# Last cross attention of a four-layer stack on one core: exponentials in a ring of six units, products with the values by halves behind later scores

## The reference, cut to what matters

```python
def _L3_xattn_ref(input, encoded_features, Wq, bq, Wkv, bkv, Wo, bo):
    B, T, E, H = (2, 256, 128, 16)
    D = E // H
    b, tq, _ = input.shape
    tk = encoded_features.shape[1]
    q = (input @ Wq + bq).reshape(b, tq, H, D).transpose(0, 2, 1, 3)
    kv = (encoded_features @ Wkv + bkv).reshape(b, tk, 2, H, D).transpose(2, 0, 3, 1, 4)
    k, v = (kv[0], kv[1])
    scores = jnp.einsum('bhqd,bhkd->bhqk', q, k) / math.sqrt(D)
    attn = jax.nn.softmax(scores, axis=2)
    out = jnp.einsum('bhqk,bhkd->bhqd', attn, v)
    out = out.transpose(0, 2, 1, 3).reshape(b, tq, H * D)
    return out @ Wo + bo
...
x = x + jnp.tanh(g_xattn[3]) * _L3_xattn_ref(_layernorm(x, axis=-1), ctx_1024, L3_xattn_Wq, ...)
```

## Time and profile before

| | |
|---|---|
| median of 3 runs | 1386.9 us (1382.16 to 1395.86) |
| the profiled execution: its own time | 1379.55 us |
| its span in the profile | 1377.7 us |
| TensorE's granted clock over the span | 0.972 of full speed |
| PE busy | 1249.3 us (91%) |
| DVE busy | 977.7 us (71%) |
| ACT busy | 932.6 us (68%) |
| POOL busy | 741.9 us (54%) |

### The profile page before, as it was taken

One profiled execution on the slowest core, in us unless ns is written; L12 is line 12 of the kernel. 1 busy time (PEld: TensorE's weight loads), 2 busy tenths in 40 slices (PEclk: granted clock), 3 DMA queues, 4 the chain that ended last, 5 costly groups with the idle time before them and its releaser, 6 DMA issues. The chain is left out here.

```text
span 1377.7 us, 44878 instructions
## 1 busy us (share of the span) xinstructions
PE 1249.3 (91%) x17964; PEld 892.8 (65%) x17964; DVE 977.7 (71%) x2439; ACT 932.6 (68%) x2297; POOL 741.9 (54%) x749
## 2 busy tenths in 40 slices
PE   6999977999999999999999999999868798998777
PEld 5777635676776677677667776777656656675443
DVE  3666657888888888788878888888743544654657
ACT  5777755677777777777777777777646665554971
POOL 3444437888878878787878778788710001003100
PEclk9999999999999999999999999999998998999998
DMA  4000032222225223422342234222302000000000
GB/s 198 1 2 1 1 115 69 67 61 59 63 61 144 58 62 78 126 59 63 82 116 59 65 80 122 58 63 70 80 2 100 1 1 27 1 0 1 1 1 16
DMA packets 68319, 76.95 MB, mean 56 GB/s; under 512 B 14864, under 2 KB 62992, under 8 KB 67600
## 3 DMA queue, kind: packets, MB, share of 16 engines
q1 hardware_dynamic: 68112, 74.07, 20.2%
HBM read 26.31 MB, written 0.52 MB: 19 GB/s over the span
## 5 line engine op out<-in xcount | busy, mean ns | idle before, releaser
L1047 POOL TENSOR_TENSOR arena<-arena,small 128x512 f32<-128x512 f32 x96 | 100.1, 1043 | 151.4 <-DVE small L930 151.4
L795 ACT ACTIVATE arena<-banks 128x512 f32<-128x512 f32 x96 | 57.4, 598 | 145.7 <-PE banks L653 145.4
L906 DVE TENSOR_TENSOR arena<-banks,rotary 128x512 f32<-128x512 f32 x192 | 131.6, 686 | 30.0 <-ACT arena L765 17.2
L1022 POOL TENSOR_TENSOR arena<-arena 128x512 f32<-128x512 f32 x96 | 122.6, 1277 | 36.5 <-DVE arena L908 36.4
L702 PE MATMUL banks<-arena 64*64 64x32 f32 x6144 | 113.2, 221 | 16.4 <-issue 8.6
L1027 POOL TENSOR_TENSOR arena<-arena 128x512 f32<-128x512 f32 x96 | 122.6, 1277 | 0.4 <-DVE arena L908 0.4
L702 PEld LDWEIGHTS banks<-arena 64*64 64x64 f32 x6144 | 101.2, 136 | 26.7 <-ACT arena L817 12.1
L503 POOL TENSOR_TENSOR arena<-arena,small 128x512 f32<-128x512 f32 x64 | 66.5, 1039 | 88.2 <-DVE small L437 88.2
L616 PE MATMUL banks<-slot,z 128*128 128x512 f32 x192 | 101.1, 608 | 6.9 <-DVE arena L908 3.6
L717 PE MATMUL banks<-arena,slot 128*128 128x128 f32 x768 | 104.2, 279 | 2.1 <-ACT arena L825 1.9
L1034 POOL TENSOR_TENSOR arena<-arena,small 128x512 f32<-128x512 f32 x96 | 100.4, 1046 | 2.0 <-ACT small L805 2.0
(11 more groups left out here) (308 smaller groups left out, 3339.3 us busy)
## 6 DMA issues: line engine op xcount, KB each, us to landing
arena<-arena SPq DMA_DIRECT2D x576, 64.0 KB
slot<-in_pack_dram SPq DMA_DIRECT2D x28, 339.5 KB, 3.5
arena<-arena SPq DMA_DIRECT2D x288, 32.0 KB
slot<-in_pack_dram SPq DMA_DIRECT2D x2, 2713.5 KB, 8.9
slot<-in_pack_dram SPq DMA_DIRECT2D x1, 3333.0 KB, 11.4
slot<-in_pack_dram SPq DMA_DIRECT2D x1, 2316.5 KB, 10.6
slot<-in_pack_dram SPq DMA_DIRECT2D x4, 337.0 KB, 4.1
slot<-in_pack_dram SPq DMA_DIRECT2D x7, 158.0 KB
```

The costliest lines, as they stand in the source:

```text
L906: e.tensor_tensor(rot, made, cos, ALU.mult)
L1022: e.tensor_tensor(m.rot_q[u % ROTS], m.rot_q[u % ROTS], m.sin_q[u % 2], ALU.add).then_inc(s["q_added"], 1)
L1047: e.tensor_tensor(p, p, stretch(m.local_small[u % 4][:, 16:24], SPAN), ALU.subtract).then_inc(s["lowered"], 1)
```

## The change

The number of units between scores and products goes from 2 to 3 (`LAG3`), the copy of a finished batch stands six units behind instead of four (`KEEP3`), the exponentials go into a ring of six units in slot 0, and the products of a pair are issued by halves: tile i = 0 of the keys (four matmuls) in step n = 2p + 4 behind the scores of unit 2p + 4, and tile i = 1 in step 2p + 5 behind the scores of unit 2p + 5. The number of instructions that compute is the same. The exponentials of unit n >= 6 wait for the products of the pair that held the buffer (`s3_o` of pair (n - 6) // 2).

```diff
-LAG3, KEEP3 = 2, 4
+RING3, LAG3, KEEP3 = 6, 3, 6
...
-def weights3(m, b, w):
-    part = (m.t_w[b][:, 0:1024], m.t_w[b][:, 1024:2048], m.t_w[b][:, 2048:3072], m.t_v[b])[w % 4]
+def weights3(m, n):
+    part = m.slots[0][:, n % RING3 * 1024:(n % RING3 + 1) * 1024]
...
-    for n in range(UNITS3 + LAG3):
+    for n in range(UNITS3 + LAG3 + 1):
...
-        if n >= LAG3 and (n - LAG3) % 2:
-            b, j, pair, w = unit3_of(n - LAG3)
+        if n >= LAG3 + 1:
+            v = n - LAG3 - 1 - (n - LAG3 - 1) % 2
+            i = (n - LAG3 - 1) % 2
+            b, j, pair, w = unit3_of(v)
...
-            for i in range(NT):
-                for g in range(GROUPS):
-                    made = e.matmul(out[32 * g:32 * g + 32, :], vz[:, i, g, j, :], weights3(m, b, w - 1 + g // 2)[:, g % 2, i, :],
-                                    start=(j == 0 and i == 0), stop=(j == 3 and i == NT - 1), skip_group_check=True)
-            made.then_inc(s["s3_o"], 1)
+            for g in range(GROUPS):
+                made = e.matmul(out[32 * g:32 * g + 32, :], vz[:, i, g, j, :], weights3(m, v + g // 2)[:, g % 2, i, :],
+                                start=(j == 0 and i == 0), stop=(j == 3 and i == NT - 1), skip_group_check=True)
+            if i == NT - 1:
+                made.then_inc(s["s3_o"], 1)
...
-        p, least, total = weights3(m, b, w), m.s3_least[n % 4], m.s3_total[n // 2 % 4]
+        p, least, total = weights3(m, n), m.s3_least[n % 4], m.s3_total[n // 2 % 4]
         e.wait_ge(s["s3_least"], n + 1)
-        if j >= 2:
-            e.wait_ge(s["s3_o"], 4 * b + j - 1)
+        if n >= RING3:
+            e.wait_ge(s["s3_o"], (n - RING3) // 2 + 1)
```

## The result

The changed kernel is slower: 1403.25 us (median of 6 runs, 1401.69 to 1407.82) against 1385.18 for the kernel before (6 runs, 1379.18 to 1395.86). The ratio is 1.0132, 95% interval 1.0092 to 1.0171.

What follows compares the result with a forecast made beforehand. A loop made by the order in PE's list, 3.87 us per pair, was taken to bound the last cross attention; 1.8 at the start plus 3.4 in the steady part gave 1386.9 - 5.2 = 1381.7 us, range 1374 to 1391.

Steps and rivals of the forecast that it cites:

- What bounds the kernel before: Last cross attention: a loop through PE's and DVE's lists, 3.87 us per pair against ACT's 3.61, 0.26 to gain.
- Buffers: Exponentials' ring in slot 0: waits for products met in time, no stall, and the tile's other place costs nothing.
- path to a maximum: From a unit's last exponential through scores to maximum: 2.6 us against ACT's 3.61 for two units, 1.0 early.
- products behind scores: PE's list, each step: scores 1.09, then a half product 0.54 to 0.74; 1.7 us allowed against ACT's 1.81.
- Rival C: PE the limit: a shape change costs 0.25 us more than allowed, pair 4.4, 7 slower, median 1394; chance 0.05.
- What is late next: DVE's maximum of the odd unit behind reciprocal and scaling: equal with ACT within 0.02, pair 3.61 to 3.63 us.
- the copy: ACT's copy of a finished batch delays the next exponential by 0.31 us, three times, 0.93 in all.
- the sum: Whole stretch: 1.8 us at the start plus 3.4 in the steady part, 5.2 gained; least 2.9, most 5.7.
- The start: First units, at the lower clock: unit 6 begins at 1279.9 instead of 1281.73, 1.8 us gained.
- the steady part: From 1281.73 to the last pair's start: 47.91 us becomes 44.49, 3.4 gained, 1.5 of it the low-clock pair.
- Rival D: TensorE's clock falls in several pairs or the layer behind; three stretches eat 4.5 us, median 1386.2; chance 0.08.
- The range: Median between 1374 (profiled time less 5.7) and 1391 us (slowest run less 5.2).

Runs made afterwards that it cites:

- the filled run: Changed kernel with three full matmuls (128x128, 512 columns) in PE's pause ahead of unit 3's scores: 1375.92 us, ratio 0.9933 to the kernel before.

## Why the prediction was wrong, step by step

- **What bounds the kernel before: right.** The loop through PE's list, with 0.26 us per pair to gain, is what the filled run shows: 3.87 became 3.60 to 3.70, and the chain runs through the exponentials.
- **Buffers, path to a maximum, products behind scores: right at full clock.** PE's step was allowed 1.7 us and took 1.07 + 0.64 = 1.71; the tail behind four products, which I had put at 0.2 from no row, is 0.64 - 0.54 = 0.10. The change of shape from scores to products, of which the earlier trace rows showed only the other direction, costs nothing beyond that. The Trainium skill, "TensorEngine Tiling (Array Packing)", Key Properties, says that changing the tiling mode drains the TensorE. No run shows the drain apart; whatever it costs is within the 1.71. Rival C, built on it, has no place in the result. Its number, 1394, was nearest to the measured one and for the wrong reason.
- **What is late next, and the copy: right.** 3.61 to 3.66 was forecast and 0.31 for the copy; the filled run has 3.65 on average and 3.90 to 3.91 with the copy, 0.25 more. Its twelve pairs from unit 6 on take 44.52 us, the sum said 44.49; from first to last exponential it takes 58.53, the sum said 64.04 - 5.2 = 58.8.
- **The start: wrong at the low clock that it assumed.** The sum has unit 6 begin 1.8 us sooner after the first exponential than before. The first two pairs did gain 1.9, but the third, the first one at the low clock, took 6.05, and unit 6 began 13.33 us after the first exponential against 12.97: 0.4 lost. The reason is the size named in the next point. In the filled run, at full clock, it is 10.87, a gain of 2.1. That the clock falls there was said, and it did.
- **The step that failed** is in the steady part: "If the clock falls again, a step costs 1.62 + 0.97 = 2.6 us instead of 1.81 for about a step and a half, 1.2 us, against a reserve of 1.0: nearly hidden". Two things in it are wrong. The size: 1.62 in the earlier trace rows is two units of scores side by side, with the clock rising within; I took it for one unit. The count in the row says so: x16, where a unit leaves 8 records. A unit alone takes 2.01, and with the half products, 1.01, a step is 3.02. And the length: I took it over from the kernel before, whose order is another. There the low stretches of the earlier trace rows ended after a few us, and I treated that as a property of the chip; here it lasted to the end of the stretch, all 13 pairs, 2.4 us each over 3.63.
- **Rival D** named the clock, but priced it at 1.5 us for each of three stretches, and argued that "PE is as busy in less time", so the clock should be safe. The low level is no matter of pauses alone: PE was busy for 83.60 of 84 us and had no pause. The Trainium skill, "TensorE: Matmul & The Clock Gate", section What's actually happening, says that "the default state is throttled, and activity releases the throttle". The run with six full matmuls in a row agrees. But an engine that is busy by the profile's measure is not thereby released from it: with one full matmul in each step PE was busy for 20.00 of 20.00 us at 0.50.
- **The range**, 1374 to 1391, came from the spread of the runs and from small costs at full clock, and slower by over 1% had a chance of 0.03. The measured 1403.25 lies 12 us above it. The case "this order at the low clock" was never worked out; from 2.6 us per step alone it would have been 5.2 per pair, 16 x (5.2 - 3.87) = 21 us more; with the measured 6.04 over 13 pairs it is 28.

What stays open: why units of scores that run alone hold the clock low; how much the number of changes adds; and what lets the clock fall, or keeps it low for three pairs, in the old order, where PE's pauses of 1.67 us may do what the lone units do here. The last was not tried. Theory P says what keeps this order low; it does not say that two units side by side are always enough to bring the clock back.

## What to carry to other kernels

When a reordering takes the pauses out of TensorE's list, work out its pace at the lower clock too: if small matmuls that ran side by side now run alone, it has two paces, and one pause decides which. Keep matmuls on different row strips next to each other, so that they overlap when PE is behind; and fill a pause ahead of such a stretch with full matmuls: here three of them fitted into the pause at the start, and the kernel before was no slower with them (ratio 0.998). That took away the fall at that place, not the later ones. Read the granted clock of each stretch before taking a duration from it, and never carry the length of a low stretch from one order to another.

## What the runs showed of the hardware

- One order of matmuls had two lasting paces: 3.63 us per pair at full clock, 6.04 at the lower, with PE busy for 83.60 of 84 us in the second. Behind a pause of 3.77 us it went from the first to the second; in another run six full matmuls of 512 columns in a row took it from the second to the first.
- A unit of scores (four matmuls on two of four row strips, 256 columns) takes 1.07 us at full clock and 2.01 at the lower, where two units on different strips together take 2.1: the second is free, if it is ready to run when the first starts. One after the other they took 3.90.
- A single product matmul between two units of scores costs 0.99 us in the chain at the lower clock, four side by side 1.01.
